# GpSimd takes thirteen of the 32 C products of a row in a selective-scan and MLP block

## The reference

```python
xx = silu(conv1d(x @ in_w.T))                    # 512 channels
delta, B, C = split(xx @ xproj_w.T)              # 16 states
delta = softplus(delta @ dt_w.T + dt_b)
for t in tokens:                                 # per channel d, state n
    h[d, n] = exp(delta[t, d] * A[d, n]) * h[d, n] + delta[t, d] * B[t, n] * xx[t, d]
    y[t, d] = sum_n h[d, n] * C[t, n]
y = (y + xx * D) * silu(res)
x = layernorm(x + y @ out_w.T)
h = silu(x @ w1) * (x @ w2); h = gelu(h @ h1); h = gelu(h @ h2)
x = layernorm(x + h @ w3)
```

## Time and profile before

| | |
|---|---|
| runs | 2984.62, 2986.29, 2989.06 us |
| profiled execution | 2989.11 us, of it 2987.1 us span |
| one row in the steady state (row 8, scan 0 to the next row's scan 0) | 170.22 us |
| busy in that row: TensorE, VectorE, ScalarE, GpSimd | 151.69, 156.25, 134.69, 87.48 us |
| granted TensorE clock, mean | 0.928 |

### The profile page before, as it was taken

One profiled execution on the slowest core, in us unless ns is written; L12 is line 12 of the kernel. 1 busy time (PEld: TensorE's weight loads), 2 busy tenths in 40 slices (PEclk: granted clock), 3 DMA queues, 4 the chain that ended last, 5 costly groups with the idle time before them and its releaser, 6 DMA issues. The chain is left out here.

```text
span 2987.1 us, 36784 instructions
## 1 busy us (share of the span) xinstructions
PE 2517.6 (84%) x12290; PEld 1881.9 (63%) x12290; DVE 2529.1 (85%) x2497; ACT 2186.1 (73%) x3335; POOL 1394.2 (47%) x1476
## 2 busy tenths in 40 slices
PE   4345798898989889898989989898989989898888
PEld 1223567675766767576666757576676757666767
DVE  3578989999898999989899989989888998989740
ACT  2767687786969788796968779696877869696721
POOL 0112444554544554454555455454455546454554
PEclk7565899999999999999999999999999999999999
DMA  1898779888888988888888979888887878888933
GB/s 55 252 307 194 176 185 208 194 207 196 208 199 195 207 194 208 192 210 193 194 203 195 208 190 212 196 209 202 189 202 186 209 194 211 197 199 200 224 114 116
DMA packets 230128, 584.84 MB, mean 196 GB/s; under 512 B 26017, under 2 KB 26401, under 8 KB 229809
## 3 DMA queue, kind: packets, MB, share of 16 engines
q0 software_dynamic: 73728, 268.47, 49.0%
q1 hardware_dynamic: 119344, 246.86, 23.9%
q10 hardware_dynamic: 36864, 67.13, 7.7%
HBM read 281.93 MB, written 31.98 MB: 105 GB/s over the span
## 5 line engine op out<-in xcount | busy, mean ns | idle before, releaser
L793 DVE TENSOR_TENSOR_SCAN scan_ps<-dA,scan_ps 128x1024 f32<-128x1024 f32 x512 | 1170.5, 2286 | 124.8 <-PE scan_ps L387 123.6
L972 POOL DMA_DIRECT2D y<-hC x512 | 452.1, 883 | 1180.7 <-DVE hC L803 1137.8
L387 PE MATMUL scan_ps<-ident,dB 128*128 128x128 f32 x4096 | 586.9, 290 | 243.9 <-DVE hC L803 220.2
L639 ACT ACTIVATE dB<-duT,bT 128x512 f32<-128x512 f32 x1024 | 724.7, 711 | 83.6 <-PE scan_ps L387 83.6
L387 PEld LDWEIGHTS scan_ps<-ident,dB 128*128 128x128 f32 x4096 | 497.4, 149 | 391.5 <-DVE hC L803 174.4
L630 ACT ACTIVATE dA<-delta,a_neg 128x512 f32<-128x512 f32 (+1 forms) x1024 | 710.2, 712 | 34.4 <-DVE hC L803 33.1
L803 DVE TENSOR_TENSOR hC<-scan_ps,c_rows_sb 128x1024 f32<-128x1024 f32 x512 | 622.8, 1216 | 94.8 <-DMA y<-hC 79.6
L501 PE MATMUL ffn_ps<-hb_hi,ring 128*128 128x512 f32 x1536 | 656.4, 427 | 34.6 <-POOL hb_lo L1011 24.2
L501 PE MATMUL ffn_ps<-hb_lo,ring 128*128 128x512 f32 x1536 | 612.9, 399 | 0.0
L501 PE MATMUL ffn_ps<-ha_hi,ring 128*128 128x512 f32 x1024 | 436.6, 426 | 4.1 <-POOL ha_lo L1011 4.1
L501 PE MATMUL ffn_ps<-ha_lo,ring 128*128 128x512 f32 x1024 | 402.8, 393 | 0.0
(11 more groups left out here) (89 smaller groups left out, 2978.2 us busy)
## 6 DMA issues: line engine op xcount, KB each, us to landing
y<-hC POOLq DMA_DIRECT2D x512, 512.0 KB, 5.7
ring<-split_weights SPq DMA_DIRECT2D x704, 256.0 KB, 4.3
c_rows_sb<-c_rows ACTq DMA_DIRECT2D x256, 256.0 KB, 4.0
xt<-x_tok SPq DMA_DIRECT2D x32, 512.0 KB, 5.6
x<-ffn_w SPq DMA_DIRECT2D x22, 512.0 KB, 10.6
split_weights<-ha_hi SPq DMA_DIRECT2D x22, 512.0 KB, 5.0
split_weights<-ha_lo SPq DMA_DIRECT2D x22, 512.0 KB, 8.9
out_tok<-out_st SPq DMA_DIRECT2D x16, 512.0 KB, 2.9
```

The source lines that it names most:

```text
L387: mm = nc.tensor.transpose(dst[:, j * P:(j + 1) * P], src(j), ident[:])
L639: nc.scalar.activation(dB[:, n % 2, t, :], duT[:, t, :], ACT.Copy, scale=bT2[:, par, t, n:n + 1]).then_inc(dB_ready, 1)
L793: nc.vector.tensor_tensor_scan(b, dA[:, a:a + 2, :].rearrange("p a l -> p (a l)"), b, 0.0, ALU.mult, ALU.add).then_inc(scan_done, 1)
L972: pool.dma_start(y2[:, par, c:c + 2, :], hC[:, p % 2], accum_op=ALU.add).then_inc(y_added[p % 2], 16)
```

## The change

Thirteen pairs of a row are now "on GpSimd". For them VectorE's scan writes the states into the `hC` slot in SBUF instead of over `scan_ps`, VectorE does no product, and GpSimd multiplies the slot in place by the C row before it issues the addition. `hC` has four slots. A VectorE product, or a scan that writes a slot, waits for the addition of pair `p-4`. TensorE's transposes wait for the scan of pair `p-2`, no longer its product, where that pair is on GpSimd. `load_c` waits for the products of both engines. Every step table of the diff's head gets new numbers, the decay tiles of an iteration come in written-out bursts (`EXP_COUNT`), and the ring for GpSimd's DMA descriptors has half its size.

```diff
-T_NORM = 19
+T_NORM = 18
-E_ADD = (14, 19)
+E_ADD = (13, 17)
-F_LOST = (47, 50, 52, 53)
+F_LOST = (47, 48, 50, 50)
...
+HC_SLOTS = 4
+POOL_PAIRS = (0, 6, 8, 9, 10, 12, 13, 17, 21, 24, 26, 28, 29)
+ON_POOL = [p in POOL_PAIRS for p in range(PAIRS)]
...
+        def wait_slot(eng, r, p):
+            g = r * PAIRS + p - HC_SLOTS
+            if g >= 0:
+                eng.wait_ge(y_added[g % 2], 16 * (g // 2 + 1))
...
             def scan_pair(r, p):
-                nc.vector.tensor_tensor_scan(b, dA[:, a:a + 2, :].rearrange("p a l -> p (a l)"), b, 0.0,
+                if ON_POOL[p]:
+                    wait_slot(dve, r, p)
+                    states = hC[:, (r * PAIRS + p) % HC_SLOTS].rearrange("p a l -> p (a l)")
+                else:
+                    states = b
+                nc.vector.tensor_tensor_scan(states, dA[:, a:a + 2, :].rearrange("p a l -> p (a l)"), b, 0.0,
...
             def c_pair(r, p):
+                if ON_POOL[p]:
+                    return
...
             def y_pair(r, par, p):
+                slot = (r * PAIRS + p) % HC_SLOTS
+                if ON_POOL[p]:
+                    n = p // 2
+                    pool.wait_ge(scan_done, r * PAIRS + (p + 1))
+                    pool.wait_ge(c_loaded[n % 2], r * (16 * STATES // 2) + 16 * (n // 2 + 1))
+                    nc.gpsimd.tensor_tensor(hC[:, slot], hC[:, slot],
+                                            c_rows[:, n % 2].unsqueeze(1).to_broadcast([P, 2, SEQ]), ALU.mult
+                                            ).then_inc(hC_pool, 1)
+                wait_product(pool, r, p)
...
-    nc = bacc.Bacc("TRN2", target_bir_lowering=False, num_devices=1, dynamic_dma_scratch_size=8192)
+    nc = bacc.Bacc("TRN2", target_bir_lowering=False, num_devices=1, dynamic_dma_scratch_size=4096)
```

More of the change, by code:

```diff
@@ L85 @@
 F_DBL_OUT = 40
-F_BT = 46
-F_BT_OUT = 53
+F_BT = 48
+F_BT_OUT = 50
 F_DT = (40, 41, 43, 44)
-F_PLUS = (46, 47, 48, 48)
-F_BASE = (42, 42, 43, 46)
-F_LOST = (47, 50, 52, 53)
+F_PLUS = (45, 46, 48, 48)
+F_BASE = (41, 43, 43, 45)
+F_LOST = (47, 48, 50, 50)
 F_LN = 51
@@ L94 @@
 F_DELTA_U = (53, 53, 53, 53)
-F_Y = (53, 56, 56, 62)
+F_Y = (57, 58, 58, 58)
 F_DU = (54, 55, 56, 58)
-T_XT = (62, 63)
+T_XT = (61, 63)
 SCALE_LEAD = 7
 EXP_LEAD, DA_RING = 4, 8
[L103 to L106, removed]
+EXP_COUNT = (3, 0, 0, 0, 1, 1, 1, 0, 1, 1, 2, 0, 2, 1, 1, 2, 3, 0, 0, 1, 1, 0, 0, 1, 0, 1, 3, 1, 2, 1, 1, 0, 1,
+             3, 1, 0, 1, 3, 1, 0, 1, 1, 1, 1, 1, 2, 0, 0, 1, 3, 0, 0, 2, 2, 0, 2, 0, 0, 0, 0, 1, 1, 2, 2)
 EXP_FIRST = EXP_LEAD
@@ L111, with products_upto @@
 SPLITS = 4
+HC_SLOTS = 4
+POOL_PAIRS = (0, 6, 8, 9, 10, 12, 13, 17, 21, 24, 26, 28, 29)
+ON_POOL = [p in POOL_PAIRS for p in range(PAIRS)]
+def products_upto(r, p, on_pool):
+    return r * sum(b == on_pool for b in ON_POOL) + sum(b == on_pool for b in ON_POOL[:p])
 def build(nc, x, in_wT, chan, xproj_wT, dt_wT, out_wT, ffn_w, ffn_s, w3_s, ident_in, out):
@@ L153, in build @@
         dA = sb("dA", [P, DA_RING, SEQ])
-        hC = sb("hC", [P, 2, 2, SEQ])
+        hC = sb("hC", [P, HC_SLOTS, 2, SEQ])
         ring = sb("ring", [P, RING, ENTRY_COLS], F32R)
@@ L252, in rows, with wait_product @@
             return row(0), row(1), row(-1), row(-2)
+        def wait_product(eng, r, p):
+            eng.wait_ge(hC_pool if ON_POOL[p] else hC_dve, products_upto(r, p + 1, ON_POOL[p]))
+        def wait_slot(eng, r, p):
+            g = r * PAIRS + p - HC_SLOTS
+            if g >= 0:
+                eng.wait_ge(y_added[g % 2], 16 * (g // 2 + 1))
         def main_loop(eng, iteration, *args):
@@ L399, in b_pair @@
                     pe.wait_ge(dB_ready, r * (STATES * TT) + (n + 1) * TT)
-                wait_past(pe, hC_done, r * PAIRS + (p - 1))
+                g = r * PAIRS + p - 2
+                if g >= 0 and ON_POOL[g % PAIRS]:
+                    pe.wait_ge(scan_done, g + 1)
+                elif g >= 0:
+                    wait_product(pe, *divmod(g, PAIRS))
                 for k in range(2):
@@ L620, in load_c @@
             def load_c(r, n):
-                wait_past(act, hC_done, r * PAIRS + 2 * (n - 1))
+                last = r * PAIRS + 2 * (n - 1)
+                if last > 0:
+                    wait_past(act, hC_dve, products_upto(last // PAIRS, last % PAIRS, False))
+                    wait_past(act, hC_pool, products_upto(last // PAIRS, last % PAIRS, True))
                 act.wait_ge(c_stored, r * 16 + 16)
```

37 lines of the change are left out of this document (16 added, 21 removed).

## The result

The changed kernel took 3019.75 to 3026.55 us in four runs, median 3023.72, against 2987.03 for the kernel before: a ratio of 1.0136, 95% interval [1.0114, 1.0157]. It is 37 us slower; the forecast was 2931.

A forecast was written before the change was run, and what follows sets the result against it. VectorE and TensorE bound the kernel in turn, by stretch. +1.15 - 2.95 + 0.4 - 0.8 - 1.3 = -3.5 us a row, 52.5 in fifteen rows plus about 3 in row 0, gave 2931 us against 2986.3; range 2838 to 2998.

The forecast's parts named there:

- the block: VectorE's two-input instructions wait out the rest of GpSimd's 2.5 us product; 0 to 2.5 us each, 4.8 us a row charged.
- Product 24: Stretch III: behind two splits, GpSimd's product reaches the L841 pair before product 25; +0.4 us, bounds -0.5 and +2.5.
- The norm of pair 9: VectorE drops a product, but L877 waits for GpSimd's two small instructions, so 0.17 us is won, not 1.13.
- Pair 26: Stretch IV: product and waits go, but product 26 blocks by +1.2 of a possible 2.5; sum -0.8 us, bounds -2.0 and +0.5.
- Pair 29: Behind scan 29 VectorE's instruction is queued while GpSimd's needs a semaphore, so the first slips through unblocked.
- Stretch V: Pairs 27 to 31: products 28 and 29 and 1.1 us of waits go; -1.3 us, bounds 0 and -1.34.
- Edits I cost at nothing: TensorE's wait for scans, `EXP_COUNT`, `load_c`, delayed splits and the smaller descriptor ring: each taken at 0, some with bounds.
- the second L925: Stretch I: the second residual addition, 0.6 us, is paid in pair 8.
- C: Rival: full blocks of 15.0 us a row at pairs 6, 8, 17, 24, 26, 29 make it slower, 3084 us; chance 0.12.
- A: Rival: blocks hardly bite, as L925 gets ahead or products come late; -7.0 us a row, 2878 us; chance 0.25.
- B: Rival: new tables let TensorE's lead carry over, recovering half its idle time, 9.3 us a row; 2844 us; chance 0.10.
- D: Rival: the gain and the blocks cancel; within 6 us of 2986; chance 0.05.

The follow-up runs named there:

- third experiment: The changed kernel with every step table and the decay bursts of before, thirteen products still on GpSimd: 2979.62 us, 0.9993 of the kernel before.
- tenth experiment: The changed kernel with T_NORM, E_ADD and bursts of before, and pair 9 multiplied by VectorE again: 2937.62 us, 0.9828 of the kernel before.
- second: The changed kernel with its new tables and bursts but every product on VectorE: 3061.03 us, 1.0262 of the kernel before.
- eleventh experiments: The changed kernel with T_NORM, E_ADD and bursts of before, only products 0, 6, 10, 12, 13, 17, 21, 28 on GpSimd: 2926.51 us, 0.9795.
- first experiment: Four product slots with the step tables and bursts of before, every product on VectorE: 2975.02 us, 0.9975 of the kernel before.

## Why the prediction was wrong

The error is 93 us: 6.1 us a row in the steady rows. It falls into two parts of about the same size, by the third experiment: about 50 us that the thirteen products miss even with the old tables (2980 for 2931), and 43 us of the new tables. By the table of pairs, the 6.1 us are 2.2 in pairs 0 to 9, 1.0 in 18 and 19, 1.0 in 20 to 25, 1.25 in 26 and 0.9 in 27 to 31, less 0.3 in 10 to 17.

**The step that failed first is the block.** I charged 4.8 us a row in four places; 9.9 are there. In pairs 6 and 8 the mechanism and the size were right: L953 took 2.41 and 1.85 us, 1.74 and 1.17 more than by itself, for 1.95 and 1.25 charged. Product 24 was to reach the two L869 before product 25, and did not: it held the end of an L863, some 0.45 us, so that the 0.4 us charged there is near by luck alone. Elsewhere it was wrong in three places.
- The norm of pair 9: "So 0.17 us is won". I had L877 wait 1.4 us for GpSimd (1.43 measured) and charged it no block: only instructions with two SBUF inputs were charged one, and L877 reads one SBUF tile. It is held for a whole product, since its releaser and the product stand one behind the other on GpSimd. The four L905 take 2 us more, pair 9 is 1.8 us longer, and taking that one product off gave 34 us (tenth experiment).
- Pair 26: 1.2 us charged, about 3.8 there (the four L875 take 6.4 us in row 8 and took 2.6). The "possible 2.5" was no upper bound: a split and a product stand one behind the other on GpSimd, and each holds an L875. The product alone costs the pair 2.1 us: with the same tables and the product on VectorE it takes 9.6 us, not 11.7 (second and eleventh experiments).
- Pair 29: "behind scans 17, 24 and 29 VectorE's instruction is queued and GpSimd's needs a semaphore, so the first slips through". One did and the next was caught; row 8, VectorE and GpSimd:

```profile
1664.52 4.24 DVE L886 TENSOR_SCALAR y<-y,ch 128x512 f32<-128x512 f32 x3
...
1661.91 2.55 POOL L998 TENSOR_TENSOR hC<-hC,c_rows_sb 128x1024 f32<-128x1024 f32 x1 [1.13 <-DVE hC L820]
...
1665.38 2.69 POOL L998 TENSOR_TENSOR hC<-hC,c_rows_sb 128x1024 f32<-128x1024 f32 x1
```

Three L886 take 4.24 us. Stretch V lost 0.4 us on average and not 1.3. At scan 17 nothing was caught, and pairs 10 to 17 gave -3.3 for -2.95: where no block falls the sum of relief was right.

**The second is "Edits I cost at nothing".** The tables and bursts were under that heading with bounds that held no loss from moved steps. They cost 86 us without a product on GpSimd and 43 with. The parts do not add up to that, since one covers another's wait, but each was taken back alone. `T_NORM` and `E_ADD` give 46 us: they put the addition behind scans 6 and 8, and leave the norm nothing to do while it waits. These two I had priced, in pairs 6 to 9, with 3.2 us of blocks; taken back they give 2.0 us a row there. Another 14 of the 46 us are pair 20's clock, in no term of the sum and open in its cause. The bursts give 25 us: they brought a wait of 0.9 us for a decay tile in pair 4, the "0.7 us, a few times" of the text, which cost nothing, and 0.6 us in pair 19, which did; the rest is pair 20 again. The transposes of `F_BT` showed in the order of instructions and I didn't cost them; in this kernel TensorE covers them. Why the tables cost twice as much without the products (pair 24 alone takes 2.9 us more than in the first experiment) I did not follow.

**What was right.** GpSimd's product 2.467 us (2.5 taken), its load of 118.75 us, scans into SBUF at 2.28 us, the stretches and who bounds them, the second L925, the 1.4 us wait, and the smaller descriptor ring at nothing. By the Trainium skill, "GPSIMD Engine Reference", performance versus the Vector engine, the product was an estimated 2.2 us; the trace has 2.467.

**The rivals.** C was nearest in kind: it says that the block decides from 8.3 us a row on, and 9.9 were there. It names pairs 6, 8, 26 and 29 rightly, 17 wrongly and 24 as good as wrongly, misses 9, and its price (3084) is too high, as not every block is full and some fall where TensorE bounds. It had 0.12. A, B and D are out by the time: L953 is blocked, and outside pairs 10 to 17 no stretch gained even what the forecast gave it. How far TensorE's lead carries over was not measured by itself. With the products in the right places the gain that the forecast spoke of is there, and more: 2910 and 2915 us.

## What to carry to other kernels

Before work goes to GpSimd, list for every piece which VectorE instructions can start in its 2.5 us, and count those with two SBUF inputs and the `TENSOR_SCALAR` forms from SBUF to SBUF alike, a whole piece for each that may meet it; then choose pieces that meet none. With the same tables seven well-placed products beat thirteen by 2.5%, 74 us, and do as well as eleven that leave out the two worst places (2910 and 2915 us). Look at what stands behind an instruction that releases another engine: the releaser's next instruction starts before the released one does. And price a table of steps by runs, with nothing but the table and with the table taken back under the change: here the two gave 86 and 43 us.

## What the runs showed of the hardware

- A GpSimd fill that reads nothing holds `TENSOR_SCALAR` on 128x256 float32 in SBUF (780 ns on average against 406) but not `TENSOR_TENSOR` with two SBUF inputs (684 against 677). A GpSimd product holds both (878 and 1932). `TENSOR_SCALAR` with an immediate in place of a per-partition scalar is held as well (L863, 0.86 us for 0.40); statistics of one SBUF tile are not (beside product 8 two of them take the 0.74 us that they take elsewhere).
- It seems to go both ways: GpSimd's product took 2.33 to 2.86 us, and two long ones of row 8 (2.83 in pair 26, 2.69 in pair 29) started where VectorE had an instruction of that kind under way. No run was made for this.
- The profile puts a block into the duration of the held instruction, with no idle time before it. A mean by line that is 1.7 to 2.9 times that of an instance by itself was the sign here.
- A lower granted clock on TensorE (0.71 to 0.80) makes pair 20 take 5.3 to 5.45 us for 3.75. It came in six of eleven rows of one program and in four of the kernel before, with the same idle time of TensorE ahead of it in every row of a program (2.3 and 2.0 us), and in none of a third with 2.3 us, so one row's trace does not tell what an edit did to it.
